# Vision transformer layer on one core: the last, single-image group as one softmax step of twelve heads

## What is computed

```python
q = q * rsqrt(norm(q, axis=1) + EPS)          # norms over the heads
k = k * rsqrt(norm(k, axis=1) + EPS)
dots = einsum('bhid,bhjd->bhij', q, k)
scores = softmax(dots / scale[:, None, None], axis=-1)
out = einsum('bhij,bhjd->bhid', scores, v)    # then out @ w_out.T + b_out
```

## Time and profile before

| what | value |
|---|---|
| median of 3 runs | 153.62 us (153.37 to 154.25) |
| the profiled execution | 155.1 us, its span 153.1 us |
| TensorE busy (PE) | 143.2 us, 94% |
| TensorE weight loads (PEld) | 129.2 us, 84% |
| VectorE busy (DVE) | 105.7 us, 69% |
| ScalarE busy (ACT) | 96.2 us, 63% |
| GpSimd busy (POOL) | 87.1 us, 57% |
| units 10 and 11 (softmax of the single image) | about 76 to 93 us of the span |

### The profile page before, as it was taken

The page is one execution under the profiler, slowest core; times in us unless marked ns, Lnnn a source line. Parts: engine busy times, 40 slices in busy tenths (PEclk is TensorE's granted clock), DMA queues, the critical chain, the costliest instruction groups (busy, mean ns, idle before and its releaser), DMA issues. The chain is left out here.

```text
span 153.1 us, 3286 instructions
## 1 busy us (share of the span) xinstructions
PE 143.2 (94%) x1172; PEld 129.2 (84%) x1172; DVE 105.7 (69%) x251; ACT 96.2 (63%) x224; POOL 87.1 (57%) x101
## 2 busy tenths in 40 slices
PE   6999799899989899999989999999999999999960
PEld 2789699899966579887968898999999998999950
DVE  0035889139587889979877536679769698678852
ACT  3054986896579796867689997425356734544541
POOL 7700369282447775999988475755735434433502
PEclk9999999999999999999999999999999999999999
DMA  4999999810033000303300000000000000000021
GB/s 135 318 378 226 229 279 242 246 40 4 0 103 105 2 4 2 103 4 103 103 4 0 4 2 0 2 4 0 0 0 0 4 0 0 0 6 0 0 65 51
DMA packets 4511, 10.60 MB, mean 69 GB/s; under 512 B 592, under 2 KB 1424, under 8 KB 4496
## 3 DMA queue, kind: packets, MB, share of 16 engines
q1 hardware_dynamic: 4496, 10.41, 24.2%
HBM read 9.96 MB, written 0.44 MB: 68 GB/s over the span
## 5 line engine op out<-in xcount | busy, mean ns | idle before, releaser
L446 POOL TENSOR_TENSOR reg_r<-reg_p,reg_r 128x324 fp32r<-128x324 f32 (+1 forms) x23 | 18.8, 821 | 21.2 <-ACT reg_r L690 21.2
L375 POOL TENSOR_TENSOR reg_w<-stage,reg_w 128x768 fp32r<-128x768 f32 x12 | 21.9, 1835 | 12.6 <-DVE reg_q L870 4.5
L690 ACT ACTIVATE reg_r<-reg_p 128x324 fp32r<-128x324 f32 (+1 forms) x24 | 10.6, 443 | 24.0 <-DVE reg_p L1032 24.0
L1032 DVE SCALAR_TENSOR_TENSOR reg_p<-reg_q 128x324 f32<-128x324 f32 (+1 forms) x24 | 14.2, 591 | 2.2
L1009 DVE TENSOR_SCALAR reg_q<-ps,bup 128x324 f32<-128x324 f32 (+1 forms) x24 | 12.3, 513 | 4.9 <-PE ps L1241 4.6
L1237 PE MATMUL ps<-reg_r,reg_w 128*128 128x324 f32 (+1 forms) x48 | 14.9, 311 | 0.0
L1238 PE MATMUL ps<-reg_r,reg_w 128*128 128x324 f32 (+1 forms) x48 | 14.2, 296 | 0.0
L1240 PE MATMUL ps<-reg_r,reg_w 128*128 128x324 f32 (+1 forms) x48 | 14.2, 295 | 0.0
L1241 PE MATMUL ps<-reg_r,reg_w 128*128 128x324 f32 (+1 forms) x48 | 14.2, 295 | 0.0
L1239 PE MATMUL ps<-reg_r,reg_w 128*128 128x324 f32 (+1 forms) x48 | 14.1, 294 | 0.0
L508 ACT ACTIVATE reg_w<-stage 128x768 fp32r<-128x768 f32 x13 | 10.9, 841 | 4.5 <-DMA stage<-w_gu_a 1.8
(11 more groups left out here) (211 smaller groups left out, 459.2 us busy)
## 6 DMA issues: line engine op xcount, KB each, us to landing
reg_x<-xw_in SPq DMA_DIRECT2D x5, 416.0 KB, 6.3
stage<-w_gu_a SPq DMA_DIRECT2D x4, 384.0 KB, 6.7
stage<-w_gu_b SPq DMA_DIRECT2D x8, 192.0 KB, 3.6
stage<-w_qkv_a SPq DMA_DIRECT2D x3, 384.0 KB, 9.9
stage<-w_qkv_b SPq DMA_DIRECT2D x6, 192.0 KB, 9.4
stage<-w_down SPq DMA_DIRECT2D x3, 384.0 KB, 3.2
wout<-w_out SPq DMA_DIRECT2D x1, 576.0 KB, 13.1
reg_x<-xw_in SPq DMA_DIRECT2D x1, 272.0 KB, 2.8
```

Source lines behind the costliest of these rows:

```text
L375: nc.gpsimd.tensor_tensor(dst[:, 1, :], raw, f(dst[:, 0, :]), ALU.subtract).then_inc(s_wlop, 1)
L446: nc.gpsimd.tensor_tensor(acts[:, n % NACT, 1, 0:w], act_f[:, n % 4, 0:w], f(acts[:, n % NACT, 0, 0:w]), ALU.subtract).then_inc(s_alo, 1)
L1032: nc.vector.scalar_tensor_tensor(out=act_f[:, n % 4, 0:w], in0=glu[:, n % 4, 0:w], scalar=GLU_LIMIT, in1=upw[:, n % 4, 0:w], op0=ALU.min, ...
```

## The change

The single image becomes one unit of twelve heads: `NU` is 11, and unit 10 holds all heads of group 5. It has no mask product, six heads in each of its two score banks, one maximum instruction over both banks, the maximum added by two identity matmuls, one exponential over both banks, one sum, reciprocal, scaling, evacuation each of twice the width, and 12 transposes and 12 products with V in a row. The former step 11 is dissolved: `logits(2)`, `gate_up(0, (0,))`, `weighted(8)`, `p_transpose(9)` on TensorE, `choose(1)`, `o_evac(8)`, `pt_evac(9)` on ScalarE, `read_logits(2)`, `rank(2)` on VectorE and `gap_exp(2)` on GpSimd now follow the loop. The expert units swap their bank pairs: unit 0 now takes over banks 2 and 3, which unit 9 leaves. On ScalarE `w_hi(13)` goes ahead of `o_evac(9)`, and `expert(1)` ahead of `o_evac(10)`.

```diff
 NG = len(SIZES)
-NU = 2 * NG
+NU = 2 * NG - 1
 TSIZES = [GRP, GRP, GRP, 124, 128]
...
 NE = HB + 1
+HL = 2 * HB
 LN_EPS, NORM_EPS = 1e-5, 1e-8
...
         mx_r = sb("mx_r", [128, 2, 6], f32r)
+        mx12 = sb("mx12", [SEQ, H], f32r)
+        psum12 = sb("psum12", [SEQ, H])
+        rinv12 = sb("rinv12", [SEQ, H])
         psum_e = sb("psum_e", [128, 2, 6])
...
+        def e_done(u):
+
+            return NE * (u + 1) if u < NU - 1 else NE * (NU - 1) + 1
+
         def s_bank(u):
...
         def e_bank(n):
-            return 2 * (place(n) % 2)
-
-        Z_BANK0 = 2 * (Z0_AT % 2)
-        Z_BANKS1 = (2, 3)
+            return 2 * ((place(n) + 1) % 2)
+
+        Z_BANK0 = 2 * ((Z0_AT + 1) % 2)
+        Z_BANKS1 = (0, 1)
...
+            def probs_last():
+
+                pool.wait_ge(s_rinv, NU)
+                pp = probabilities(NU - 1)[0:SEQ, 0:H * SEQ].rearrange("p (h j) -> p h j", h=H)
+                nc.gpsimd.tensor_tensor(pp, pp, rinv12[:, :].unsqueeze(2).to_broadcast([SEQ, H, SEQ]),
+                                        ALU.mult).then_inc(s_p, 1)
+
             def root(g, n, ve, done):
...
             for k in range(0, NU):
-                probs(k)
+                if k < NU - 1:
+                    probs(k)
+                else:
+                    probs_last()
                 if k == 4:
...
                     w_lo({3: 8, 5: 9, 6: 10, 8: 11, 10: 12}[k])
+            gap_exp(2)
             w_lo(13)
...
+            def exps_last():
+
+                u = NU - 1
+                act.wait_ge(s_pt, u - 2)
+                act.wait_ge(s_sub, u + 1)
+                b = s_bank(u)
+                nc.scalar.activation(probabilities(u)[0:SEQ, 0:H * SEQ].rearrange("p (b n) -> p b n", b=2),
+                                     ps[0:SEQ, b:b + 2, 0:HL * SEQ], ACT.Exp).then_inc(s_e, 1)
+
             def pt_evac(u):
                 n = SIZES[u // 2]
+                w = (HB if u < NU - 1 else HL) * n
                 act.wait_ge(s_pt, u + 1)
...
                     act.wait_ge(s_pv, u - 1)
-                nc.scalar.activation(PT[0:n, u % 2, 0:6 * n].rearrange("p (b n) -> p b n", b=2),
-                                     ps[0:n, 4:6, 0:HB * n], ACT.Copy).then_inc(s_ptev, 1)
+                nc.scalar.activation(PT[0:n, u % 2, 0:2 * w].rearrange("p (b n) -> p b n", b=2),
+                                     ps[0:n, 4:6, 0:w], ACT.Copy).then_inc(s_ptev, 1)
...
                     act.wait_ge(s_op, 1)
-                nc.scalar.activation(o_tiles(g)[:, 3 * j:3 * j + 3, :],
-                                     ps[:, O_BANK, 0:HB * n].rearrange("p (m n) -> p m n", m=3), ACT.Copy)\
+                w = HB if u < NU - 1 else HL
+                nc.scalar.activation(o_tiles(g)[:, w * j:w * j + w, :],
+                                     ps[:, O_BANK, 0:w * n].rearrange("p (m n) -> p m n", m=w), ACT.Copy)\
                     .then_inc(s_oev, 1)
...
                     h1_evac(2)
-                exps(k)
+                if k < NU - 1:
+                    exps(k)
+                else:
+                    exps_last()
                 if k == 0:
...
                     w_hi({3: 9, 5: 10, 7: 11}[k])
-                if k == 11:
-                    choose(1)
                 if k >= 3:
...
                     w_hi(8)
+            choose(1)
+            o_evac(8)
+            pt_evac(9)
             nc.scalar.preload_act_table_set("gelu_apprx_sigmoid_and_others")
+            w_hi(13)
             o_evac(9)
             pt_evac(10)
-            w_hi(13)
             w_hi(14)
...
             choose(2)
+            expert(1)
             o_evac(10)
-            pt_evac(11)
-            expert(1)
             expert(2)
-            o_evac(11)
             h1_evac(3)
...
                 if u >= 2:
-                    dve.wait_ge(s_e, NE * (u - 1))
+                    dve.wait_ge(s_e, e_done(u - 2))
                 b = s_bank(u)
-                nc.vector.reduce_max(mx_r[0:n, u % 2, :].rearrange("p (b h) -> p b h", b=2),
-                                     ps[0:n, b:b + 2, 0:HB * n].rearrange("p b (h j) -> p b h j", h=HB),
+                h = HB if u < NU - 1 else HL
+                dst = mx_r[0:n, u % 2, :] if u < NU - 1 else mx12[:, :]
+                nc.vector.reduce_max(dst.rearrange("p (b h) -> p b h", b=2),
+                                     ps[0:n, b:b + 2, 0:h * n].rearrange("p b (h j) -> p b h j", h=h),
                                      X, negate=True).then_inc(s_mx, 1)
...
                 n = SIZES[u // 2]
-                dve.wait_ge(s_e, NE * (u + 1))
+                dve.wait_ge(s_e, e_done(u))
                 nc.vector.reduce_sum(psum_e[0:n, u % 2, :],
...
                 nc.vector.reciprocal(rinv[0:n, u % 2, :], psum_e[0:n, u % 2, :]).then_inc(s_rinv, 1)
+
+            def sum_recip_last():
+
+                dve.wait_ge(s_e, e_done(NU - 1))
+                nc.vector.reduce_sum(psum12[:, :],
+                                     probabilities(NU - 1)[0:SEQ, 0:H * SEQ].rearrange("p (h j) -> p h j", h=H),
+                                     X).then_inc(s_sum, 1)
+                dve.wait_ge(s_sum, NU)
+                nc.vector.reciprocal(rinv12[:, :], psum12[:, :]).then_inc(s_rinv, 1)
...
                     h1_lo(2)
-                sum_recip(k)
+                if k < NU - 1:
+                    sum_recip(k)
+                else:
+                    sum_recip_last()
                 if k == 7:
...
                     ln1(k // 2 - 2)
-                if k in (9, 11):
+                if k == 9:
                     read_logits(k // 2 - 3)
...
                     router_weights(k // 2 - 4)
+            read_logits(2)
+            rank(2)
             dve.wait_ge(s_rows, 2)
...
                 else:
-                    pe.wait_ge(s_e, NE * (u - 1))
+                    pe.wait_ge(s_e, e_done(u - 2))
+                if u == NU - 1:
+                    pe.wait_ge(s_qn, g + 1)
+                    pe.wait_ge(s_kn, g)
+                    for m in range(NP):
+                        for i in range(2):
+                            r = slice(64 * i, 64 * i + 64)
+                            last = mm(ps[0:n, b + i, m * n:(m + 1) * n], qk[r, m, o:o + n], qk[r, NP + m, o:o + n],
+                                      start=(m == 0), stop=False, skip_group_check=True)
+                    last.then_inc(s_s, 1)
+                    return
                 for i in range(2):
...
                 pe.wait_ge(s_mx, u + 1)
+                if u == NU - 1:
+                    for i in range(2):
+                        last = mm(ps[0:n, b + i, 0:HL * n], ident_r[0:n, 0:n],
+                                  mx12[:, HL * i:HL * i + HL].unsqueeze(2).to_broadcast([n, HL, n]),
+                                  start=False, stop=True, skip_group_check=True)
+                    last.then_inc(s_sub, 1)
+                    return
                 mm(ps[0:n, b + 1, 0:HB * n], ident_r[0:n, 0:n],
...
                 pe.wait_ge(s_p, u + 1)
+                w = HB if u < NU - 1 else HL
                 for i in range(2):
-                    for m in range(3):
+                    for m in range(w):
                         last = nc.tensor.transpose(ps[0:n, 4 + i, m * n:(m + 1) * n],
-                                                   probabilities(u)[0:n, (3 * i + m) * n:(3 * i + m + 1) * n], ident[0:n, 0:n])
+                                                   probabilities(u)[0:n, (w * i + m) * n:(w * i + m + 1) * n], ident[0:n, 0:n])
                 last.then_inc(s_pt, 1)
...
                     pe.wait_ge(s_lg, (u - 3) // 2)
-                for m in range(3):
+                w = HB if u < NU - 1 else HL
+                for m in range(w):
                     for i in range(2):
-                        c = 128 * (3 * j + m) + 64 * i
+                        c = 128 * (w * j + m) + 64 * i
                         last = mm(ps[64 * i:64 * i + 64, O_BANK, m * n:(m + 1) * n], V[0:n, g, c:c + 64],
-                                  PT[0:n, u % 2, (3 * i + m) * n:(3 * i + m + 1) * n], start=True, stop=True)
+                                  PT[0:n, u % 2, (w * i + m) * n:(w * i + m + 1) * n], start=True, stop=True)
                 last.then_inc(s_pv, 1)
...
                 n, o = TSIZES[g], TOFFS[g]
-                pe.wait_ge(s_oev, (2, 4, 6, 10, 12)[g])
+                pe.wait_ge(s_oev, (2, 4, 6, 10, 11)[g])
                 if g == 0:
...
                 if n < 2 and 0 in parts:
-                    pe.wait_ge(s_e, NE * (NU - 1 + n))
+                    pe.wait_ge(s_e, e_done(NU - 2 + n))
                     pe.wait_ge(s_h1lo, 6)
...
                     h1_transpose(2)
-                if k == 11:
-                    logits(2)
-                    gate_up(0, (0,))
                 if k >= 3:
...
                     logits(k // 2 - 3)
+            logits(2)
+            gate_up(0, (0,))
+            weighted(8)
+            p_transpose(9)
             gate_up(0, (1,))
...
```

(2 more changed lines are left out.)

## The result

The changed kernel takes 152.98 us (median of 12 runs), the kernel before 153.87 us beside it; the ratio is 0.9917 with a 95% interval of 0.989 to 0.9943, so 0.8% or 1.3 us faster. A second comparison gave 0.9915 (0.9884 to 0.9946). The 152.98 us lie inside that range only because the kernel before, too, came out slower beside them, at 153.87; as a ratio, 0.9917 of 153.62 is 152.34 us and lies outside. The direction was right and the size was not.

A forecast was written before the change was run, and what follows sets the result against it. TensorE was taken to bound the kernel, dense behind `h1_transpose(2)`. Gains of 0.16 + 0.09 + 0.09 + 0.11 = 0.45 us off 153.62 gave 153.15 us, own range 152.75 to 153.5, 8-of-10 range 152.6 to 153.8.

The forecast's parts named there:

- the anchor: Start of `h1_transpose(2)` at 79.78 us, released by VectorE after 0.35 us idle; TensorE savings ahead of it count nothing.
- `subtract_max(11)`, 0.16 us: On TensorE behind the anchor, before `logits(2)`: removing this instruction gains 0.16 us, bounds 0 and 0.16.
- The two merged blocks, 0.09 us each: Single image on TensorE: twelve transposes in one block, and twelve products with V in one, gain 0.09 us each.
- The wait of `w_transpose(0)`, 0.11 us: TensorE behind `h1_transpose(3)`: the wait for the last `o_evac` goes, gaining 0.11 us, bounds 0 and 0.2.
- The bounds: Limits on the gains behind the anchor: 0 to 0.16 us, 0 to 0.2 us, and lower bound 0 for both blocks.
- The costs put at nothing: Extra score heads, identity products and wider maximum ahead of the anchor, swapped banks, and `w_hi(13)` moved on ScalarE: cost 0.
- The chain behind `w2_lo(0)`: Expert stretch: `spread(0)` needs `w2_lo(0)`; that chain comes forward 0.4 us, TensorE 0.45 us, so it still fits.
- a new wait in the expert stretch: Sign to look for: a wait in the expert work not there before would prove the prediction wrong altogether.
- The table load: ScalarE, softmax tail: load starts near 85.0 us instead of 85.55, takes 1.28 us; the present trace shows no extra drain.
- The rivals: Four alternatives: 152.8 us (chance 0.16), 153.5 (0.12), 154.3 (0.08), and 153.35, sharing 0.64 with the forecast.
- the first: Rival: the 0.35 us wait at the anchor shrinks too, as VectorE reaches unit 9's sum earlier; 152.8 us, chance 0.16.
- The slower rival: `project(3)` waits for `o_evac(9)` behind `w_hi(13)` on ScalarE; 0.65 us slower than before, 154.3 us, chance 0.08.

The follow-up runs named there:

- the one with the wait of 1.54 us: Changed kernel with VectorE's `ln1(2)` ahead of `sum_recip(9)` and `h1_lo(2)` ahead of `read_logits(1)` and `rank(1)`; ratio 1.013 to the kernel before.
- the repeated experiment: Changed kernel with one unread 36 x 36 x 108 product between `p_transpose(8)` and `logits(2)`, run again; `logits(2)` came 1.93 us behind `h1_transpose(2)`.

## Why the prediction came out too small

- **What bounds the kernel, and the anchor**: right. `h1_transpose(2)` is released by VectorE at 35.57 us in both kernels, its wait grew from 0.35 to 0.56 us (I had said 0.4 to 0.7), and the mask alone is worth nothing. `spread(0)`, though, came 0.82 us earlier behind the anchor (15.51 to 14.69) and not 0.45: the sum behind the anchor was half of what it should have been, and this is where the prediction failed.
- **`subtract_max(11)`, 0.16 us**: the step that failed first, and the largest error. I took the distance from its start to the next instruction. Its cost also lies ahead of it: the transposes before it run to the next start in 0.54 us when `logits(2)` follows, and in 0.70 us when the small product follows. It measured 0.32 us.
- **The two merged blocks, 0.09 us each**: 0.11 and 0.12 us, nearly right.
- **The second block of small products as a neighbour**: missing in the sum altogether. Without it `h1_transpose(3)` starts 0.09 us sooner behind `gate_up(2)`, and its second transpose 0.05 us sooner, together 0.14 us.
- **The wait of `w_transpose(0)`, 0.11 us**: the reason was right and the size was half. The transpose itself comes 0.16 us sooner and `gate_up(3)` behind it another 0.06 us, together 0.22 us. I had read the wait off the products; the weight loads of the same trace name it, with 0.23 us.
- **The sum** by what was measured: 0.32 + 0.11 + 0.12 + 0.14 + 0.22 = 0.91 us, where I had 0.45.
- **The bounds** were too tight as well. The upper bounds that I gave (0.16 and 0.2, and 0.09 for each block) add up to 0.54 us, or 153.08 us; the 152.75 us with which my range for the forecast began do not follow from them. My value for the small product went no further than its own start-to-start distance; a better one from the same trace was at hand, the whole 0.86 us from the start of `p_transpose(8)` to `logits(2)` less the 0.54 us that the same six transposes take ahead of `gate_up(0)` one step later. That gives the 0.32 us. The two lines of the kernel before, one step later:

```profile
83.63 0.77 PE L1376 MATMUL ps<-ident,reg_p 108*108 108x108 f32 x6
84.17 0.40 PE L1237 MATMUL ps<-reg_r,reg_w 128*128 128x324 f32 x1
```

- **The costs put at nothing** (twelve-head scores, two identity products, the wide maximum, the banks, `w_hi(13)`): all at nothing. The chain behind `w2_lo(0)`, of which I had said that it still fits, did not quite: it delays `spread(0)` by 0.1 us. I had called a new wait in the expert stretch a proof that I was wrong altogether; this one is worth nothing, as `spread(1)` gives it back. `project(3)` was forecast 87.73 - 79.78 = 7.95 us behind the anchor and starts 7.75 us behind it; 0.16 us of the difference is the other half of the small product, the rest some hundredths in the transposes and behind `logits(2)`.
- **The table load**: the Trainium skill, ScalarE: Activation LUTs, section What ACT_TABLE_LOAD costs, gives a drain of about 1380 ns with each switch. The changed kernel, too, shows none: the load starts at 83.34, and the next instruction at 84.63.
- **The rivals**: none came true as told. The time of the first (152.8 us) was near, but its mechanism, an earlier `h1_transpose(2)`, didn't happen. The slower rival's place is shown by added work: 0.75 us more ahead of the copy made `project(3)` 0.61 us late.

## What to carry to other kernels

The cost of a small instruction on a dense TensorE is the distance between its two neighbours with it, less their distance without it, found at another place of the same trace where like neighbours stand side by side; its own start-to-start distance held only half here (0.16 of 0.32 us). Small blocks (products of 36 rows here) are best run as one row: cutting one in two between full-size ones cost 0.57 us here. And where a wait is released by an engine that has idled just before, look at what is queued there: moving two short VectorE steps (`ln1(2)` and `read_logits(1)`, four instructions) ahead of one sum, with `w_hi(13)` back in its old place, gave 0.39 us more in the trace.

## What the hardware showed that I had not expected

A 36-row product among full-size ones costs 0.25 to 0.32 us where one of 108 rows costs 0.05 to 0.12, with little difference by its columns, and a row of three costs 0.10 us more than one.

The granted clock is more easily lost than I had thought. It fell to 1.2 GHz within the work of four of the traces, in all three with small products added between `p_transpose(8)` and `logits(2)` and in the one with the wait of 1.54 us. In the others it fell only at the end, behind TensorE's last product (in the changed kernel that product starts at 145.76 us, and the fall is at 149.00). The busy time by stretch of the repeated experiment, ahead of the fall and in it:

```profile
77.70:81.10 3.40, 2.84 (x29) 2.10 (x29) 3.15 (x16) 2.60 (x6) 2.57 (x3) 1.00 0.00 0
81.10:84.50 3.40, 3.40 (x22) 2.80 (x22) 1.99 (x8) 2.13 (x8) 3.40 (x3) 0.51 0.00 0
```

TensorE was busy for 2.84 of the 3.40 us before it, with one wait of 0.6 us. The changed kernel has the same wait and, in its trace, full clock throughout the softmax and expert stretches. What tips it was not settled: three of the four had added small products behind a wait of about 0.6 us, the fourth a wait of 1.54 us and no added product. Eight traces, two of the changed kernel and six of kernels built from it, had the wait of 0.56 us and no small product at that place, and kept the clock there. A trace shows one execution only, so this does not show that they always keep it.
